# State-space stage: identity multiplications on TensorE between the steps of the prologue

## The reference

```python
xn = layer_norm(x, ln_g, ln_b)
xz = xn @ in_proj_w
u, z = (xz[..., :Din], xz[..., Din:])
u = silu(depthwise_causal_conv(u, conv_w, conv_b))
dbc = u @ x_proj_w
dt, Bm, Cm = dbc[..., :8], dbc[..., 8:24], dbc[..., 24:40]
delta = softplus(dt @ dt_proj_w + dt_proj_b)
y = selective_scan(u, delta, -exp(A_log), Bm, Cm, D)
out = (y * silu(z)) @ out_proj_w
return residual + out
```

## Time and profile before

| | |
|---|---|
| median of 3 runs | 2700.87 us (2694.35 to 2701.8) |
| the profiled execution | 2705.45 us, its span 2703.7 us |
| mean granted clock of TensorE | 0.931 |
| busy: TensorE, VectorE, ScalarE, GpSimd | 2405.5, 2045.3, 1513.5, 301.9 us |

### The profile page before, as it was taken

How to read it: one execution, slowest core, us unless ns; L and a number is a source line. 1 busy time by engine, 2 the same in 40 slices (tenths; PEclk the granted TensorE clock), 3 DMA queues, 4 the chain that set the end, 5 groups by cost and what they waited for, 6 DMA issues and landing times. The chain is left out here.

```text
span 2703.7 us, 33636 instructions
## 1 busy us (share of the span) xinstructions
PE 2405.5 (89%) x10214; PEld 876.6 (32%) x10272; DVE 2045.3 (76%) x3008; ACT 1513.5 (56%) x1842; POOL 301.9 (11%) x333
## 2 busy tenths in 40 slices
PE   6888677999999979999586599999999999997998
PEld 3555411222222224444222133323333333332443
DVE  5676688999995224344697888989999998976775
ACT  5555486777677843333332576666666666653111
POOL 5665500000000000000164000000000000000000
PEclk8898957999999989999698599999999999998998
DMA  5354371221000159954124331122013111111100
GB/s 144 127 167 143 130 113 31 67 63 31 26 24 27 31 104 211 217 153 121 32 73 98 78 91 30 30 63 72 29 30 105 30 30 30 30 36 69 47 1 8
DMA packets 200960, 198.63 MB, mean 73 GB/s; under 512 B 18525, under 2 KB 159362, under 8 KB 200086
## 3 DMA queue, kind: packets, MB, share of 16 engines
q1 hardware_dynamic: 200674, 196.69, 28.1%
q10 hardware_dynamic: 144, 0.10, 0.0%
HBM read 152.01 MB, written 41.48 MB: 72 GB/s over the span
## 5 line engine op out<-in xcount | busy, mean ns | idle before, releaser
L2768 DVE TENSOR_TENSOR y_acc<-y_acc,y_probs 128x1024 f32<-128x1024 f32 x400 | 486.7, 1217 | 35.2 <-ACT y_probs L2456 23.1
L2456 ACT ACTIVATE y_probs<-y_E,y_mask_bias 128x1024 f32<-128x1024 f32 x408 | 433.7, 1113 | 71.9 <-PE y_E L2548 63.9
L1223 ACT ACTIVATE x_probs<-x_E 128x1024 f32<-128x1024 f32 x408 | 397.1, 1024 | 135.8 <-PE x_E L1283 133.6
L1406 DVE TENSOR_REDUCE x_maxima<-x_M 128x1 f32<-128x496 f32 x660 | 410.2, 668 | 27.8 <-PE x_M L1265 17.2
L2557 PE MATMUL y_O<-y_probs,y_values 128*64 128x512 f32 x1632 | 400.2, 611 | 0.0
L2547 PE MATMUL y_E<-y_qa,y_ks 128*128 128x512 f16 x816 | 313.4, 384 | 1.5 <-ACT y_copied L2429 1.2
L2548 PE MATMUL y_E<-y_qb,y_ks 66*128 66x512 f16 x816 | 311.6, 382 | 0.0
L2429 ACT ACTIVATE y_copied<-y_M 128x1024 bf16<-128x1024 f32 (+1 forms) x164 | 162.5, 991 | 212.7 <-PE y_M L2511 212.7
L2706 DVE TENSOR_REDUCE y_maxima<-y_M 128x2 f32<-128x1024 f32 (+2 forms) x195 | 231.2, 1185 | 41.3 <-PE y_M L2511 32.3
L1874 DVE TENSOR_TENSOR f_hidden<-f_act_out,f_spread 128x512 f32<-128x512 f32 x160 | 110.7, 692 | 176.0 <-ACT f_act_out L1705 106.1
L1296 PE MATMUL x_O<-x_probs,x_values 128*32 128x512 f32 x1632 | 218.1, 607 | 0.7 <-ACT x_probs L1223 0.4
(11 more groups left out here) (499 smaller groups left out, 3154.6 us busy)
## 6 DMA issues: line engine op xcount, KB each, us to landing
f_spread<-comb_dram SPq DMA_DIRECT2D x160, 256.0 KB, 7.0
y_values<-v_dram SPq DMA_DIRECT2D x208, 128.0 KB, 2.2
v_dram<-a_v_out SPq DMA_DIRECT2D x26, 512.0 KB, 2.6
k_dram<-a_k_parts SPq DMA_DIRECT2D x26, 512.0 KB, 3.4
x_values<-v_dram SPq DMA_DIRECT2D x100, 128.0 KB, 2.2
f_weights<-f_w_in SPq DMA_DIRECT2D x40, 256.0 KB, 10.1
y_ks<-k_dram SPq DMA_DIRECT2D x75, 128.0 KB, 2.9
ssm_c_rows<-c_dram SPq DMA_DIRECT2D x16, 512.0 KB, 3.6
```

Source lines behind the costliest of these rows:

```text
L1223: nc.scalar.activation(probs[:, n % 2, 2 * g:2 * g + 2, :], psE[:, 2 * g:2 * g + 2, :], ACT.Exp).then_inc(exped, 1)
L1406: V.tensor_reduce(maxima[:, 2 * h + j, qt, c:c + 1], psM[(2 * entry + j) % 3][:, 0:CHUNK0], AX.X, ALU.max).then_inc(max_done, 1)
L2456: A(probs[:, i, :], psE[:, 2 * (i % 2):2 * (i % 2) + 2, :].rearrange("p a b -> p (a b)"), ACT.Exp, bias=mask_bias[:, bass.ds(c * TILES_IN_ ...
L2768: ins = V.tensor_tensor(acc[:, u % 2, :], acc[:, u % 2, :], probs[:, i, :], ALU.add)
```

## The change

TensorE gets a helper `stay_busy(bank, times)`, which multiplies the identity with the input weights `in_proj` (128x512) into the first half of a PSUM tensor, so many times. Nothing reads the result: the tensor is written anew (with `start=True`) before its next use. The calls stand at these places of TensorE's list: 4 into `B[2]` behind the bias multiplications; 4 into `B[1]` before each half of the x-projection; 2 into `B[1]` behind it; and 37 into `B[3]` behind the spread of state 0, in eleven groups, each behind a wait for a step of softplus or for the first drive. The wait for `z_done` before the first spread goes; waits for `copied` come, which guard the tensors written.

```diff
+                def stay_busy(bank, times):
+
+                    for _ in range(times):
+                        T.matmul(B[bank][:, 0:512], ident[:], in_proj[:], start=True, stop=True)
+
                 for c in range(4):
                     ins = T.matmul(B[3][:, c:c + 1], in_proj[:, P * c:P * c + P], ln_b[:], start=True, stop=True)
                 ins.then_inc(S["bias_mm"], 1)
+                stay_busy(2, 4)
...
                 e.wait_ge(S["load"], 16 * LOADS)
+                e.wait_ge(S["copied"], 1)
                 for j in range(CH):
+                    stay_busy(1, 4)
                     e.wait_ge(S["silu_done"], j + 1)
...
                 ins.then_inc(S["dbc_mm"], 1)
+                stay_busy(1, 2)
                 e.wait_ge(S["dbc_done"], 1)
...
                 e.wait_ge(S["load_sel"], 16)
-                e.wait_ge(S["z_done"], CH)
...
                 spread_b(0, 0)
+                e.wait_ge(S["copied"], 3)
+                for name, count, times in (("z_done", 1, 3), ("z_done", 2, 3), ("exped", 1, 3), ("exped", 2, 3), ("lned", 1, 3),
+                                           ("lned", 2, 3), ("inved", 1, 3), ("inved", 2, 3), ("soft", 1, 6), ("soft", 2, 3),
+                                           ("driven", 1, 4)):
+                    e.wait_ge(S[name], count)
+                    stay_busy(3, times)
                 for n in range(STATES - 1):
                     next_state(n, n % 2, first=(n == 0))
```

## The result

The changed kernel takes 2713.6 us (median of 7 runs, 2706.62 to 2716.05) against 2700.87 us (7 runs, 2694.35 to 2705.39): a ratio of 1.0047, with a 95% interval of 1.0029 to 1.0065. It is 12.7 us, or 0.47%, slower; the forecast was 9.5 us, and the range 2701.5 to 2717.5 holds the measured time.

What follows compares the result with a forecast made beforehand. VectorE bounds the state loop; TensorE arrives 10.6 us late, plus 3.4 for a clock fall, so the second drive is 9.9 us late. Less the third drive's 0.39 us wait: +9.5 on 2700.87, 2710.4 us, range 2701.5 to 2717.5.

Steps and rivals of the forecast that it cites:

- The sign: Whole kernel: slower, 9.5 us or 0.35%; chances slower 0.65, same 0.32, faster 0.03.
- The first block: Four multiplications before the transposes: 5.2 us (3.4 to 6.9), delaying the in-projection's first chunk by half a microsecond.
- The stream: In-projection through the 37: 130 passes of 0.43 us without a wait, 55.9 us, plus 3.4 for one clock fall.
- Softplus 2.2 us earlier: Prologue: dt-projection through at 1315.9 instead of 1318.1 us, moving the softplus chain forward 2.2 us.
- The loop: Loop over the states: third drive's 0.39 us wait goes; VectorE, without slack, cannot catch up the second drive's delay.
- no fall: Rival, around the 8- and 40-row work: same overrun without the clock fall's 3.4 us, +6.1 us, 2707.0; chance 0.25.
- The 37 fit: Rival, last block: its passes fit the gap before the loop, leaving the clock's gain, -7.0 us, 2693.9; chance 0.06.
- The block stays at 1.2 GHz: Rival, last block: identity multiplications don't raise the clock, 74 passes take 63.6 us, about +38 us, 2739; chance 0.05.

Runs made afterwards that it cites:

- e1: Changed kernel with 18 instead of 37 multiplications in the last block, at the same waits; 2700.75 us, ratio 0.9994 to the kernel before.
- e2: Changed kernel without the last block of 37 and its waits, the 14 earlier multiplications kept; 2702.5 us.
- e6: Changed kernel with dt weights, B selection and dbc padded with zeros, so the same multiplications use 128 rows; 2704.0 us.
- e5: Changed kernel with all 51 added multiplications kept in place, each with 256 columns instead of 512; 2699.2 us.
- e10: Kernel before plus 128-row padding (weights' zeros in memory, dbc cleared at the stage's start) and 28 multiplications cut to the gaps; 2693.21 us, ratio 0.9974.

## Why the prediction was right

The sign, the mechanism and the place were those of the forecast: TensorE streams from the in-projection to the end of the 37 without a wait, is late for the second B row, and the second drive waits 14.64 us (about 14 were named). That this wait came out so near is partly luck: the second drive came 4.2 us later than forecast, and the first drive, behind whose scans the wait begins, 3.5 us later. The sum came out small, 9.5 us against 12.7 by the medians, just inside its upper end of 12.9, and 15.5 in the traced stage, outside it. By its terms, counted from the stage's start:

- **The first block.** The in-projection started 12.6 us after the stage's start; the forecast had 11.4. The block took 6.62 us and not the middle of its bounds, 5.2, because the clock rose only at its end. In e1 and e2 it took 5.22 and 5.25. The term was sized within its bounds, and this execution lay near the upper one.
- **The stream.** 62.2 us against 55.9 + 3.4. The passes and their 0.43 us held. The fall took 10.2 us, the upper row that was named, and cost 5.1 us, not the middle 3.4; of the remaining 1.2 us, some 0.8 are joints between the blocks ahead of dt, which I had counted at nothing (the 44 passes from 1291.51 on make 18.9 us at 0.43, and dt starts 19.7 us behind); where the other 0.4 lie was not found.
- **Softplus 2.2 us earlier** did not come: the second bias addition ended 38.5 us after the stage's start, 1.3 later than before (37.2), since the late first block moved all that follows and dt took 4.97 us when the clock fell in it. This cost nothing, since TensorE was later still.
- **The loop.** The third drive's 0.39 us wait went, as foreseen, but dips of the clock put 0.84 and 0.65 us elsewhere; the loop took 99.2 us against 98.9. That the loop has dips by chance of the execution was missing from the sum. A last one (1463.7 to 1467.1) fell into the last accumulation, which holds up the end of the stage; from the last drive to the end the stage took 18.2 us against 17.1.

These add up: 1.3 + 2.9 us make the second drive 14.1 us later instead of 9.9; with 0.3 in the loop and 1.1 behind it the stage is 15.5 us longer.

Of the rivals, *no fall* was wrong: the clock fell in every trace that had the 8- and 40-row work behind high-clock streaming. It is also where the Trainium skill's page "TensorE: Matmul & The Clock Gate", section "Why this matters for your kernels", was weighed: it names idle gaps as what brings the clock down. The traces do not agree that this is all. The stream had no gap and the clock fell for 10.2 us; e6 shows that the rows made the difference. *The 37 fit* was right in its mechanism and wrong in its size; e1 and e5 are that case, and their second drive waits for nothing. The gain of 7.0 us that it named did not come with the fit alone, though (stages of 177.9 and 180.8 us against 178.8), but only with the padding beside it (e10, 170.1). *The block stays at 1.2 GHz* did not occur: 29.8 us of the block ran at 1.00.

## What to carry to other kernels

Work added to hold TensorE's clock is free only as long as it ends before the next real input: add up its passes at the traced cadence, with a fall of the clock on top, against the gap, since everything past it lands on whoever waits for TensorE next. Before adding work, look at the rows of the work that is there: where few rows of the array are in use, padding with zeros cost no pass here and held the clock while TensorE streamed; what it does cost is the clearing or loading of the zeros. A version that did both, with blocks cut to the gaps, was 0.26% faster than the kernel before (interval 0.07 to 0.44%), where the 51 of the change were 0.47% slower.

## What the runs showed of the hardware

The granted clock fell to 0.50 while TensorE was busy without a gap, in 8-row multiplications (at 1313.5 us), stayed there through the 40-row ones and 3.9 us of the 128-row ones behind them (to 1323.7), and stayed at 1.00 through the same passes with 128 rows (e6). The 40-row B rows are what lets it dip in the loop: 98.9 to 107.2 us from the second to the last drive with 40 rows (nine traces), 97.8 with 128 (five traces). And a GpSimd clearing of SBUF beside VectorE's normalization nearly doubled the latter, 4.11 us against 2.13. The Trainium skill's page "SBUF — State Buffer", section "Who interferes with whom", says that GpSimd and VectorE's two-port instructions, `tensor_scalar` among those that can be, hold one shared pair of ports by turns, and the trace agrees: the longest of the eight normalization instructions took 1.90 us and ended with the last clearing, at 1290.3, and the four behind it took 0.33 us each. That the one was locked out by the other was not shown by itself.
